# Second attention of a gated two-layer block on one NeuronCore: contexts by 32-column tiles of TensorE, already transposed, all sixteen heads in one place of the step

## The reference

```python
scores = jnp.einsum('bhsd,bhnd->bhsn', Q, K) / SCALE
topk_scores, topk_indices = jax.lax.top_k(scores, 32)
sparse_weights = jax.nn.softmax(topk_scores, axis=-1)
context = jnp.einsum('bhsk,bhskd->bhsd', sparse_weights, sel_V)
context = context.transpose(0, 2, 1, 3).reshape(B, S, D_MODEL)
return context @ Wo.T + bo
```

## Time and profile before

| | |
|---|---|
| median of 3 runs | 828.84 us (827.23 to 830.07) |
| the profiled execution | 835.15 us, of which its span is 833.4 us |
| mean granted clock of TensorE | 0.911 |
| loop step | 38.8 us, ten times; steps 5 and 16 look like one |
| PE busy over the span | 727.6 us (87%) |
| DVE busy over the span | 595.7 us (71%) |
| ACT, POOL busy | 460.3 us, 450.7 us |

### The profile page before, as it was taken

The page is one execution under the profiler, slowest core; times in us unless marked ns, Lnnn a source line. Parts: engine busy times, 40 slices in busy tenths (PEclk is TensorE's granted clock), DMA queues, the critical chain, the costliest instruction groups (busy, mean ns, idle before and its releaser), DMA issues.

```text
span 833.4 us, 17983 instructions
## 1 busy us (share of the span) xinstructions
PE 727.6 (87%) x4442; PEld 579.3 (70%) x4442; DVE 595.7 (71%) x3758; ACT 460.3 (55%) x1226; POOL 450.7 (54%) x696
## 2 busy tenths in 40 slices
PE   3589998899999999999999999999999966763696
PEld 3467666677877777877777777777777845552696
DVE  2544633878888888888888888888877888993232
ACT  2137455676767575767676676757574724221222
POOL 6076554465556565655657555556574544653153
PEclk8579999999999999999999999999997975555798
DMA  7200069960000000000000000000000000100682
GB/s 190 57 0 1 1 171 297 307 186 2 1 2 2 0 0 0 0 0 0 0 0 0 0 0 0 0 0 0 0 1 1 2 0 1 45 26 33 199 224 68
DMA packets 38531, 37.85 MB, mean 45 GB/s; under 512 B 3632, under 2 KB 34247, under 8 KB 38482
## 3 DMA queue, kind: packets, MB, share of 16 engines
q1 hardware_dynamic: 32984, 27.76, 12.2%
q10 hardware_dynamic: 3994, 6.36, 3.0%
q0 software_dynamic: 1504, 3.17, 1.1%
HBM read 16.28 MB, written 21.45 MB: 45 GB/s over the span
## 4 chain that ended last, share of the span: by engine, by line
PE 54%; DVE 22%; issue 9%; ACT 5%; POOL 3%; SPq 3%; DMA 1%; another core or an unknown queue 1%; DVEq 0%; POOLq 0%; ACTq 0%
PE bank L849 9%; DVE raw L1533 9%; PE bank L720 8%; DVE m L1527 6%; PE bank L876 4%; PE bank L866 4%; PE bank L837 4%; PE bank L867 4%; PE bank L918 3%; PE bank L935 3%; DVE negmax L1475 3%; PE bank L1155 3%; ACT prob L1183 2%; PE bank L1165 2%; PE bank L898 2%
## 5 line engine op out<-in xcount | busy, mean ns | idle before, releaser
L1533 DVE MATCH_REPLACE8 raw<-m,raw 128x77 f32<-128x77 f32 x1024 | 221.4, 225 | 0.0
L1527 DVE MAX8 m<-raw 128x8 f32<-128x77 f32 x1024 | 190.4, 228 | 1.0 <-DVE raw L1533 0.6
L1183 ACT ACTIVATE prob<-bank,negmax 128x205 f32<-128x205 f32 x256 | 108.3, 428 | 129.6 <-DVE negmax L1475 129.3
L514 POOL TENSOR_TENSOR raw<-raw,m 128x616 f32<-128x616 f32 x64 | 77.9, 1218 | 148.5 <-DVEq L1509 148.5
L495 POOL TENSOR_TENSOR prob<-prob,inv 128x820 f32<-128x820 f32 x64 | 99.5, 1555 | 73.6 <-DVE inv L1480 73.6
L849 PE MATMUL bank<-kvT,g_sb 128*128 128x205 f32 x512 | 124.6, 367 | 0.0
L1475 DVE TENSOR_REDUCE negmax<-bank 128x2 f32<-128x410 f32 x128 | 74.2, 580 | 52.1 <-PE bank L849 51.1
L849 PEld LDWEIGHTS bank<-kvT,g_sb 128*128 128x128 f32 x512 | 83.5, 191 | 10.3
L935 PEld LDWEIGHTS bank<-v,p1T 77*128 77x128 f32 x512 | 75.2, 218 | 15.1 <-issue 4.7
L1533 DVE MATCH_VALUE_LOAD raw<-m,raw 128x8 f32 x1024 | 80.4, 78 | 0.0
L935 PE MATMUL bank<-v,p1T 77*128 (+1 forms) x512 | 72.3, 269 | 8.1 <-ACT p1T L1183 3.9
(11 more groups left out here) (232 smaller groups left out, 1344.8 us busy)
## 6 DMA issues: line engine op xcount, KB each, us to landing
z_sorted<-no_row SPq DMA_DIRECT2D x1, 17415.0 KB, 64.9
b_w<-in_L_ffn_W ACTq DMA_DIRECT2D x23, 256.0 KB
z_tile<-z_sorted SPq DMA_DIRECT2D x23, 129.0 KB, 2.4
w<-in_L_ffn_W SPq DMA_DIRECT2D x8, 256.0 KB, 4.7
raw<-in_L_xattn_Wkv SPq DMA_DIRECT2D x2, 512.0 KB, 5.5
xs<-in_x SPq DMA_DIRECT2D x1, 960.0 KB, 8.1
cx<-in_ctx SPq DMA_DIRECT2D x1, 577.5 KB
raw<-in_L_xattn_Wq SPq DMA_DIRECT2D x1, 512.0 KB, 3.6
```

Of the source, the lines that this page charges most:

```text
L1183: return nc.scalar.activation(dst, src, f, **kw)
L1527: v.max(m8[:, h, r, :], sw[:, h, src, :]).then_inc(s[name], 1)
L1533: v.match_replace(sw[:, h, 1, :], m8[:, h, r, :], sw[:, h, src, :], TAKEN)\
```

## The change

- `contexts(b)` does all 16 heads at once, in slot 1 for batch E. The fixed operand is now narrow, 77 by 32, and the transposed p of a head (77 by 128) is the moving one. Four matmuls in a row (j = 0 to 3) write the partitions 32j to 32j+31 of bank M, and so use the column tiles 0 to 3 of PE. For head 4j+q only 8 of the 32 columns of the operand hold values (`v_wide`), the others zeros; the four quads q are accumulated into the same 128 columns of M.
- The denominators come from four more such matmuls for each q, with `ones_wide`, which has ones in the same 8 columns; they land in the next 128 columns of M. So there are 32 matmuls for a batch in place of 16.
- The result is already transposed. DVE takes 128 reciprocals for each partition and multiplies into `c_zT`. `context_T`, its transpose, and ACT's copy are gone; `second_out` waits for `cz_ready`.
- `p1T` now holds all 16 heads (in memory of `z_tile`, used later). POOL gets `widen_values`, a copy of 77 x 128 elements into `v_wide`, in slot 4. Five more memsets net stand at its start.
- PE's loop begins a step earlier: 5 to 15, after `before_loop`, which waits for the router's weights (`ld_router`). DVE raises `lg_ready` once before the steps, and PE's and ACT's counts of it go up by one.

```diff
+        v_wide = sb("v_wide", [NK, QUADS * (128 + D1)])
+        ones_wide = sb("ones_wide", [NK, QUADS, 32])
...
+            for q in range(QUADS):
+                g.memset(ones_wide[:, q, D1 * q:D1 * q + D1], 1.0).then_inc(s["c_const"], 1)
...
+            def widen_values(b):
+                reach(pool, "ctx_psum", b, 0)
+                w = v_wide[:, :].rearrange("p (q r) -> p q r", q=QUADS)[:, :, 0:128]
+                g.tensor_copy(w.rearrange("p q (j w) -> p q j w", j=4)[:, :, :, 0:D1],
+                              batch(v1.rearrange("p b h d -> p b (h d)"), b).rearrange("p (j q d) -> p q j d", q=QUADS, j=4))\
+                    .then_inc(s["vw_ready"], 1)
...
-            def contexts(b, q):
+            def contexts(b):
                 free("M")
-                reach(pe, "p1T_ready", b, q + 1)
-                for n in range(4):
-                    c = CT0 + (4 * q + n) * (D1 + 1)
-                    last = mm(M[:, c:c + D1 + 1], p1T[:, n, :], v1[:, bass.ds(b, 1), 4 * q + n, :].squeeze(1),
-                              start=True, stop=True)
+                reach(pe, "p1T_ready", b, QUADS)
+                reach(pe, "vw_ready", b, 1)
+                for q in range(QUADS):
+                    for n in range(2):
+                        for j in range(4):
+                            w = v_wide[:, 128 * q + 32 * j:128 * q + 32 * j + 32] if n == 0 else ones_wide[:, q, :]
+                            last = mm(M[32 * j:32 * j + 32, CT0 + 128 * n:CT0 + 128 * n + 128], w, p1T[:, 4 * j + q, :],
+                                      start=(q == 0 and n == 0), stop=(q == QUADS - 1), skip_group_check=True)
                 last.then_inc(s["ctx_psum"], 1)
...
-            def context_T(b):
-                free("M")
-                reach(pe, "cz_ready", b, 1)
-                turn(M[:, 0:128], c_z[:, :, :].rearrange("p h d -> p (h d)")).then_inc(s["cT_psum"], 1)
-                read_next("M", "cT_ready", 5, 1)
...
                         if E is not None:
-                            contexts(E, 3)
+                            contexts(E)
...
-                        if C is not None:
-                            contexts(C, 0)
...
-                        if C is not None:
-                            contexts(C, 1)
...
-                        if C is not None:
-                            contexts(C, 2)
...
+            def before_loop():
+
+                pe.wait_ge(s["ld_router"], 32)
+                free("M")
+                read_next("M", "lg_ready", 6, 2)
+
+            run_steps(pe, step, LAGS - 1, before_loop)
...
             def context_out(b):
...
-                v.reciprocal(c_inv[:, :], c[:, :, D1]).then_inc(s["cinv_ready"], 1)
+                v.reciprocal(c_inv[:, :], M[:, CT0 + 128:CT0 + 256]).then_inc(s["cinv_ready"], 1)
                 reach(dve, "cinv_ready", b, 1)
-                v.tensor_tensor(c_z[:, :, :], c[:, :, 0:D1], c_inv[:, :].unsqueeze(2).to_broadcast([128, H, D1]),
-                                ALU.mult).then_inc(s["cz_ready"], 1)
+                v.tensor_tensor(c_zT[:, :], M[:, CT0:CT0 + 128], c_inv[:, :], ALU.mult).then_inc(s["cz_ready"], 1)
```

More of the change, by code:

```diff
@@ L148, in flamingo_kernel @@
         m8 = sb("m8", [128, H, ROUNDS, 8])
-        p1T = sb("p1T", [NK, 4, 128])
-        c_inv = sb("c_inv", [128, H])
-        c_z = sb("c_z", [128, H, D1])
+        c_inv = sb("c_inv", [128, 128])
         c_zT = sb("c_zT", [128, 128])
@@ L167, in flat @@
             return sb(name, [128, n])[:, :]
-        z_tile = flat("z_tile", RING * ROW).rearrange("p (u w) -> p u w", u=RING)
+        z_flat = flat("z_tile", RING * ROW)
+        z_tile = z_flat.rearrange("p (u w) -> p u w", u=RING)
+        p1T = z_flat[0:NK, 2 * ROW:2 * ROW + H * 128].rearrange("p (h q) -> p h q", h=H)
         bf_rows = z_tile[0:2 * PST * HC, 0, 0:256]
@@ L241, in apart, with run_steps @@
             eng.sem_inc(s["waits_apart"], 1)
-        def run_steps(eng, step):
+        def run_steps(eng, step, first=LAGS, ready=None):
             def peeled(i):
                 step(i, lambda n: i - n if 0 <= i - n < NB else None)
-            for i in range(LAGS):
+            for i in range(first):
                 peeled(i)
-            with eng.Fori(LAGS, NB) as i:
+            if ready:
+                ready()
+            with eng.Fori(first, NB) as i:
                 step(None, lambda n: i - n)
@@ L332, in move_jobs @@
                     n = k - J_V1
-                    last = copy(v1[:, 4 * n:4 * n + 4, :, 0:D1].rearrange("p b h d -> p (b h) d"),
-                                src[0:NK, :].rearrange("p (h d) -> p h d", d=D1))
+                    last = copy(v1[:, 4 * n:4 * n + 4, :, :].rearrange("p b h d -> p (b h d)"), src[0:NK, :])
                 last.then_inc(done, 1)
@@ L413, in _ @@
             g.iota(token_no[:, :], pattern=[[128, NB]], base=0, channel_multiplier=1).then_inc(s["c_token"], 1)
-            g.memset(v1[:, :, :, D1:D1 + 1], 1.0).then_inc(s["c_const"], 1)
-            pool.wait_ge(s["c_const"], 6 + NE)
+            for w in (v_wide[:, :], ones_wide[:, :, :]):
+                g.memset(w, 0.0).then_inc(s["c_const"], 1)
+            pool.wait_ge(s["c_const"], 7 + NE)
+            for q in range(QUADS):
+                g.memset(ones_wide[:, q, D1 * q:D1 * q + D1], 1.0).then_inc(s["c_const"], 1)
             g.affine_select(out=ident[:, :], in_=ident[:, :], compare_op=ALU.not_equal, fill=1.0, base=0,
@@ L678, in step @@
                             keep_top(C, 2)
+                            widen_values(C)
                         if P is not None:
@@ L962, in logits @@
                 mm(M[:, 0:NE], r_zT[:, :], wr[:, :], start=True, stop=True).then_inc(s["lg_psum"], 1)
-                read_next("M", "lg_ready", 5, 1)
+                read_next("M", "lg_ready", 5, 2)
             def up_perm(st):
@@ L1063, in step @@
                             project_out(A2, 3)
-                        if E is not None:
-                            context_T(E)
                         if A is not None:
@@ L1116, in step @@
                         if E is not None:
-                            if i == 5:
-                                pe.wait_ge(s["ld_router"], 32)
                             logits(E)
@@ L1133, in step @@
                 now["step"] += 1
-            run_steps(pe, step)
+            def before_loop():
[3 more added lines that the diff above has]
+            run_steps(pe, step, LAGS - 1, before_loop)
             count_rows(2)
@@ L1257, in second_probs_out @@
                 reach(act, "p1T_psum", b, q + 1)
-                copy(p1T[:, :, :].rearrange("p h q -> p (h q)"), X[0:NK, :]).then_inc(s["p1T_ready"], 1)
+                copy(p1T[:, 4 * q:4 * q + 4, :].rearrange("p h q -> p (h q)"), X[0:NK, :]).then_inc(s["p1T_ready"], 1)
             def bias_stage(st):
@@ L1314, in step @@
                     if slot == 3:
-                        if E is not None:
-                            move(E, c_zT, "cT_psum", "cT_ready")
                         if A is not None:
@@ L1670, in _ @@
             dve.wait_ge(s["c_gate"], 1)
+            dve.sem_inc(s["lg_ready"], 1)
             run_steps(dve, step)
```

15 lines of the change are left out of this document (6 added, 9 removed).

## The result

The changed kernel takes **854.78 us** (median; 851.83 to 855.88), the kernel before 828.66 us: a ratio of 1.029 with a 95% interval of 1.0259 to 1.0322. It is slower, by 26 us. The profiled execution of the changed kernel is the quickest of its four, 851.83 us (span 849.7 us); that of before was above its median.

A forecast was written before the change was run, and what follows sets the result against it. PE and DVE were taken to hand the step to each other, the reciprocal on DVE's part; 8.4 + 2.2 - 0.35 + 2.1 + 1.5 + 3.6 = 17.5 us, added to the median 828.84, gave 846 us; range 828 to 880.

The forecast's parts named there:

- PE, removed: Old context groups, transpose of c_z and its wait: 4.04 us a step less PE work, but gain 0.
- PE, added: Slot 1's new contexts, 64 records in place of 8: a block of 2.6 us, between 2.2 and 7.5.
- 64 records start within 2.0 to 2.4 us: Sign for the profile after: the starts of the slot 1 context block on PE span that time.
- the bound 16 x 0.11 us: Context block in slot 1 with four column tiles side by side: 16 rounds, 1.76 us.
- The term of 0.2 us of wait a step: DVE waiting in slot 1 for the 2.6 us block, with 2.39 us of room; 2.2 us over 11 steps.
- DVE: 0.70 us more for the reciprocal: Slot 1's reciprocal grows from 16 to 128 elements, 250 to 950 ns; 8.4 us over 12 steps.
- The link through slot 4: First score matmul into bank X waits for ACT's p1T copy behind slot 3's exponentials and maxima, so DVE's 0.9 us reaches PE.
- The step, 39.5 to 39.9 us: Sign for the profile after: length of a loop step, against 38.80 us before; below 38.8 the prediction is wrong.
- rival 3: PE's clock: 1.3 to 1.8 us idle before slot 4's score matmul brings half clock every third step, 866 us; chance 0.15.
- The end: Last steps: 1.5 us for the half-clock block in step 19, 3.6 us in step 20.
- in-order starts: Rival: matmuls start in program order, slot 1 block of 4.0 us, 867 us; chance 0.13.
- no overlap: Rival: slot 1's column tiles do not overlap, block 7.5 us, DVE waits 5.1 us, about 924 us; chance 0.06.

The follow-up runs named there:

- run 4: Kernel before without the contexts of quads 0 to 2 (quad 3's stand in): 825.77 us, against 830.12 for the kernel before beside it.
- run 2: Changed kernel with a narrow reciprocal, 16 for each partition used 8 times over: 838.87 us, against 830.12 for the kernel before.
- run 1: Kernel before with its 16 reciprocals taken 8 times over (128 elements), nothing else changed: 844.89 us, against 830.12 for the kernel before.
- run 5: Changed kernel, ACT's copies of quad 1's numerators and slot 4's first scores ahead of slot 3's exponentials, PE forming those scores before slot 4's attention scores: 841.27 us.
- run 7: Changed kernel with only ACT's copy of quad 1's numerators moved ahead of the exponentials of slot 3: 840.68 us.
- run 8: Kernel before with only ACT's copy of quad 1's numerators moved ahead of slot 3's exponentials: 832.02 us, against 831.30 for the kernel before.
- run 9: Changed kernel with the same 32 context matmuls ordered one column tile after the other: 919.76 us, against 830.70 for the kernel before.
- run 11: Changed kernel with PE's slot 6 and ACT's GELUs reordered and ACT's copy of quad 1's numerators early: 833.34 us, against 830.70 for the kernel before.
- run 12: Run 11 with DVE's list reordered: slot 3's maxima and second residual before f_z, slot 0's maxima before b_z: 808.23 us, against 831.69 for the kernel before.

## Why the prediction was right

The time, 854.8 us, lies in the range of 828 to 880 us, and slower was the likely sign with 0.79. It lies 9 us above the forecast's 846 and just above the forecast's own range of 842 to 853. By its steps:

- **PE, removed: 0.** Right but for 0.15 us a step (run 4; and run 2 against before).
- **PE, added: a block of 2.6 us.** Too much: the last group of the block starts at 444.75 and DVE's reciprocal at 445.49 waits for nothing. "64 records start within 2.0 to 2.4 us" was 1.7. It is nearest to the bound 16 x 0.11 us that the prediction set lower; the tiles overlap fully, and the allowance for imperfect overlap was not needed. The term of 0.2 us of wait a step (2.2 us in the sum) is 0.
- **DVE: 0.70 us more for the reciprocal, all of it on the path.** Right: 0.94 us against an estimate of 0.95, and 0.67 to 0.70 us a step in runs 1 and 2.
- **The link through slot 4.** Right, but not the only one. It stands in the chain of the changed kernel; taken away (runs 5 and 7), the step did not move, since a second one from the maxima of slot 4 is as long. The prediction did not see it. For the sum that made no difference, because both begin on DVE.
- **The step, 39.5 to 39.9 us.** The undisturbed step is 39.34: 0.54 above before, by 0.70 - 0.15. For the twelve steps 5 to 16 the sum had 10.6 us; twelve times 0.54 is 6.5.
- **The clock.** This is the step of the prediction that failed. The forecast had none of it, and rival 3 had it in every third step, at up to 5 us each, with 0.15. It came in 8 of the 10 loop steps of the profile, at 1.46 us for each stretch of 3.41 us: some 13 us. The idle time itself was foreseen (1.3 to 1.8 us, measured 1.64); that it would be followed by half clock was judged by long idle times elsewhere, which stand alone.
- **The end.** Step 20 cost 2.5 us in place of 3.6, the stretch of step 19 lost 0.6 in place of 2.2: at half clock the block takes 3.2 us to the last start, and DVE waited 0.43 us for it in step 19. In step 16 the changed kernel won 3.4 us, since the 10.2 us at half clock that the profile of before has there are missing. That gain belongs to the one profile, not to the change: run 8, whose steps are those of before (38.78 us), has 3.4 us at half clock there and takes 41.43 us for the stretch, and 75.18 us for the end, where the changed kernel takes 41.17 and 75.06.

So the forecast came near partly by luck, because errors went against each other. The sum had 17.5 us. The waits in the loop and in steps 19 and 20 were too dear by some 7 us, and the 13 us of the clock were left out; that gives 23 to 24 us, against 26 between the medians. The 16.3 us between the two profiles are smaller for a part by the 5.7 us of step 16 and the end, which are the profile's own. Against run 8 in place of before, the span of the changed kernel is 21.7 us longer: 18.4 in the ten steps, 3.7 in the last three, and next to nothing elsewhere. What is left to the 26 us lies between the profiled runs and their medians. The theory behind the forecast, that this step is made of DVE's list and that a longer operation there comes through whole, is what the runs bear out best.

Of the rivals: in-order starts (block of 4.0 us) and no overlap (7.5 us) did not come. Run 9 shows what the second would look like, 920 us; the prediction had 924, which is near by luck, since it had DVE wait 5.1 us for the block and no half clock, and DVE waits 3.63 us with 1.46 us of half clock beside it. By the order of matmul starts that the Trainium skill gives in TensorE: Matmul & The Clock Gate, Part 3 (packing small matmuls), the prediction had a block of 4.0 us, with both records of a matmul started before those of the next. The trace does not agree for these 32-bit matmuls of two records each: eight records on four tiles start every 0.22 us.

## What to carry to other kernels

Ask of an operation in which engine's list it stands and whether that list is the step, not how long the engine is busy: here 2 us of PE work were worth 0.15 us a step, 0.70 us of DVE work 0.70, and letting DVE do what stood ready behind a wait 1.6. Before moving an operation ahead in a list, see whether its input is there in time: the same move on ACT was free in one kernel and cost 1.5 us a step in the other. Look at the granted clock of a step after work is taken from PE, because the freed time becomes an idle time at the next hand-over, and filling it or moving the hand-over can be worth more than the work was. Narrow tiles of TensorE pay if neighbours in the list are on different tiles, and a result that comes out repeated (each denominator eight times) is paid again by the engine that reads it.

## What was not expected of the hardware

- Of the idle times of PE, the length alone did not tell which would be followed by half clock. 1.64 us, 0.79 us of work and 0.60 us: in 8 of 10 loop steps, with the same idle times in the other two. 1.50, 0.79 and 0.60 us: in all ten (run 9). 1.07, 0.79 and 0.60 us: in 6 of 10 (run 2). 1.45 us in one piece (runs 7 and 11) and 1.54 us with the next one 8 us later (run 4): in none. 1.19 us in one piece (run 1): in the last three of ten, after seven without. And behind the 1.73 to 1.74 us of step 16 came 10.2 us at half clock before, 3.4 us in run 8, none in run 1. Two idle times close together seem to be worse than one, but runs 1 and 8 do not fit that alone; what decides stays open. The Trainium skill, TensorE: Matmul & The Clock Gate, Part 1, tells of a kernel whose clock swings because PE idles shortly between groups of matmuls as it goes through PSUM banks, and the trace here agrees in kind, at a hand-over of a PSUM bank.
- A stretch of 3.41 us at half clock costs the step 1.46 us, though only PE is slowed and DVE bounds the step: the stretch lies on the link by which PE's scores reach DVE. In the undisturbed step DVE waits 0.35 and 1.10 us for the scores of slots 5 and 6, in a disturbed one 2.00 and 0.92: together 1.47 us more.
- DVE's reciprocal goes by the element: 203, 353 and 703 ns for 8, 32 and 88 of them, 250 for 16 and 941 for 128. The line through the small ones gave the large one to 1%.
- `b_z` on DVE takes 2.28 us in the changed kernel, where POOL's product of 2.27 us runs beside it, and 0.82 us in run 12, where it begins 1.54 us after that product instead of with it. In both it ends 0.08 us behind the product, and `f_z`, an operation of the same kind and shape with no such product beside it, takes 0.35 us. The maxima ahead of it in run 12 keep their 0.58 us beside the product.
